# A head's values times both halves of its probabilities: one matmul of 512 columns in place of two of 256, and a sum on VectorE

## What is computed

```python
kv_input = jnp.concatenate([xn, ln], axis=1)
k, v = jnp.split(kv_input @ Wkv + bkv, 2, axis=-1)
sim = jnp.einsum('bhid,bhjd->bhij', q * DH ** (-0.5), k)
attn = jax.nn.softmax(sim, axis=-1)
out = jnp.einsum('bhij,bhjd->bhid', attn, v)
return out.transpose(0, 2, 1, 3).reshape(b, -1, INNER) @ Wo + bo
```

## Time and profile before

| | us |
|---|---|
| median of three runs | 1913.81 |
| profiled execution | 1916.26 |
| its span, first to last instruction | 1914.4 |
| TensorE busy | 1889.9 (99%) |
| VectorE busy | 1464.6 (77%) |
| ScalarE busy | 1221.6 (64%) |
| GpSimd busy | 392.2 (20%) |
| first half of the program | to about 1075 |

### The profile page before, as it was taken

The page is one execution under the profiler, slowest core; times in us unless marked ns, Lnnn a source line. Parts: engine busy times, 40 slices in busy tenths (PEclk is TensorE's granted clock), DMA queues, the critical chain, the costliest instruction groups (busy, mean ns, idle before and its releaser), DMA issues.

```text
span 1914.4 us, 41535 instructions
## 1 busy us (share of the span) xinstructions
PE 1889.9 (99%) x13834; PEld 1764.6 (92%) x13834; DVE 1464.6 (77%) x3620; ACT 1221.6 (64%) x2554; POOL 392.2 (20%) x610
## 2 busy tenths in 40 slices
PE   7999999999999999999999999999999999999999
PEld 6888888888888888888889899999999999999998
DVE  7877777777777776777667788888888878888776
ACT  5655565556555655565566776667777777767753
POOL 2222222222222222122255211111111111111100
PEclk9999999999999999999999999999999999999999
DMA  3021112111210000000052933433333333433400
GB/s 125 29 72 40 43 60 71 38 44 60 71 38 28 12 22 22 11 11 22 13 109 53 332 79 80 84 59 82 85 72 75 76 71 75 85 75 66 86 7 12
DMA packets 101982, 119.33 MB, mean 62 GB/s; under 512 B 39072, under 2 KB 87072, under 8 KB 101920
## 3 DMA queue, kind: packets, MB, share of 16 engines
q1 hardware_dynamic: 93216, 83.93, 14.5%
q0 software_dynamic: 8704, 34.61, 10.0%
HBM read 97.29 MB, written 21.23 MB: 62 GB/s over the span
## 4 chain that ended last, share of the span: by engine, by line
PE 93%; DVE 3%; ACT 2%; DMA 1%; issue 1%; POOL 0%; DVEq 0%; SPq 0%; POOLq 0%; ACTq 0%
PE ring L651 10%; PE ring L653 10%; PE ring L652 10%; PE ring L1935 8%; PE ring L1937 8%; PE ring L1936 8%; PE ring L707 5%; PE sim L651 3%; PE sim L653 3%; PE sim L1937 3%; PE sim L652 3%; PE sim L1935 3%; PE sim L1936 3%; PE ps_x L651 1%; PE ps_x L652 1%; PE ps_x L653 1%
## 5 line engine op out<-in xcount | busy, mean ns | idle before, releaser
L435 ACT ACTIVATE a_pr<-sim,a_nmax 128x512 f32<-128x512 f32 x256 | 173.8, 684 | 204.9 <-DVE a_nmax L566 204.9
L1935 PE MATMUL ring<-b_xch,b_wel 128*128 128x256 f32 x1024 | 289.9, 283 | 0.5 <-DVE b_act_e L1558 0.5
L1937 PE MATMUL ring<-b_xcl,b_weh 128*128 128x256 f32 x1024 | 286.5, 280 | 0.0
L1936 PE MATMUL ring<-b_xch,b_weh 128*128 128x256 f32 x1024 | 286.3, 280 | 0.0
L346 POOL TENSOR_SCALAR a_pr<-a_pr,a_rinv 128x512 f32<-128x512 f32 x256 | 185.0, 739 | 450.8 <-DVE a_rinv L576 448.0
L1936 PEld LDWEIGHTS ring<-b_xch,b_weh 128*128 128x128 f32 x1024 | 193.4, 189 | 0.0
L1935 PEld LDWEIGHTS ring<-b_xch,b_wel 128*128 128x128 f32 x1024 | 192.1, 188 | 0.7 <-DVE b_act_e L1558 0.7
L1937 PEld LDWEIGHTS ring<-b_xcl,b_weh 128*128 128x128 f32 x1024 | 192.1, 188 | 0.0
L1274 ACT ACTIVATE b_heh<-b_act_e 128x512 fp32r<-128x512 f32 x128 | 80.7, 630 | 147.0 <-DVE b_act_e L1558 113.1
L544 DVE SCALAR_TENSOR_TENSOR a_ktl<-ring,a_bkv_s,a_kth 128x512 fp32r<-128x512 f32 x128 | 95.3, 745 | 96.7 <-ACT a_kth L415 95.9
L557 DVE TENSOR_TENSOR a_ptl<-ring,a_pth 128x512 fp32r<-128x512 f32 x256 | 163.8, 681 | 1.6 <-ACT a_pth L425 0.5
(11 more groups left out here) (357 smaller groups left out, 6345.2 us busy)
## 6 DMA issues: line engine op xcount, KB each, us to landing
b_w2l_raw<-in_W2T POOLq DMA_DIRECT2D x16, 1088.0 KB, 8.6
b_even_b<-rows_between SPq DMA_DIRECT2D x16, 1024.0 KB, 5.5
b_w1l_raw<-in_W1T POOLq DMA_DIRECT2D x16, 1024.0 KB, 8.3
b_w1l_raw<-in_We SPq DMA_DIRECT2D x8, 768.0 KB, 4.5
expert_halves<-b_w1h SPq DMA_DIRECT2D x8, 768.0 KB, 3.3
expert_halves<-b_w1l SPq DMA_DIRECT2D x8, 768.0 KB, 5.6
b_weh<-expert_halves SPq DMA_DIRECT2D x8, 768.0 KB, 7.3
b_wel<-expert_halves SPq DMA_DIRECT2D x8, 768.0 KB, 8.9
```

What stands on the lines that cost most here:

```text
L435: nc.scalar.activation(pr[:, h % 2, t, :], sim[t][:], ACT.Exp, bias=nmax[:, h % 2, t:t + 1], accum_out=rsum[:, h % 2, t:t + 1]).then_inc(e ...
L1935: nc.tensor.matmul(out, ll, rh, start=(n == 0), stop=False)
L1936: nc.tensor.matmul(out, lh, rh, start=False, stop=False)
L1937: last = nc.tensor.matmul(out, lh, rl, start=False, stop=(n == len(parts) - 1))
```

## The change

The tiles `pth` and `ptl` become the two parts of one tile `pt` (P x 2 x 4 x 256). In the O fill, for each block k, `vh` is multiplied with both parts in one matmul of 512 columns into the whole bank, so that `vh x pth` lies in columns 0 to 255 and `vh x ptl` in columns 256 to 511; `vl x pth` is still a matmul of 256 columns and is added to the first part. VectorE's low half of O then has two instructions: the old one from the first part, and a sum that adds the second part to `otl`, after a wait for the first (a new semaphore `o_step`, counted up to 128).

```diff
-    pth, ptl = (of["probs"].put(n, [P, KT, S], F32R, odd=0) for n in ("a_pth", "a_ptl"))
+    pt = of["probs"].put("a_pt", [P, 2, KT, S], F32R, odd=0)
+    pth, ptl = pt[:, 0], pt[:, 1]
-    consts = sem("consts")
+    consts, o_step = sem("consts"), sem("o_step")
-        def low_half(order, i):
+        def low_half(order, i, heads=0):
             else:
                 nc.vector.scalar_tensor_tensor(otl[:, h], bank[:, 0:S], bkv_s[:, 1, h:h + 1], f32(oth[:, h]),
-                                               ALU.add, ALU.subtract).then_inc(ring_lo, 1)
+                                               ALU.add, ALU.subtract).then_inc(o_step, 1)
+                dve.wait_ge(o_step, heads)
+                nc.vector.tensor_tensor(otl[:, h], f32(otl[:, h]), bank[:, S:2 * S], ALU.add).then_inc(ring_lo, 1)
-                    low_half(order, i + j)
+                    low_half(order, i + j, b * H + h)
-                low_half(order, i)
+                low_half(order, i, b * H + H)
-                last = product(bank[:, 0:S], range(KT), lambda k: vh[h // KT][:, k, cols],
-                               lambda k: vl[h // KT][:, k, cols], lambda k: pth[:, k, :], lambda k: ptl[:, k, :])
+                wide = bank[:].rearrange("p (z s) -> p z s", z=2)
+                for k in range(KT):
+                    left = vh[h // KT][:, k, cols]
+                    if k > 0:
+                        nc.tensor.matmul(bank[:, 0:S], vl[h // KT][:, k, cols], pth[:, k, :], start=False, stop=False)
+                    last = nc.tensor.matmul(wide, left, pt[:, :, k, :], start=(k == 0), stop=(k == KT - 1))
+                    if k == 0:
+                        nc.tensor.matmul(bank[:, 0:S], vl[h // KT][:, k, cols], pth[:, k, :], start=False, stop=False)
```

## The result

The changed kernel takes 1922.51 us (median of 5 runs, 1922.11 to 1922.84), the one before 1914.66 us in the same comparison (1913.24 to 1915.64). The ratio is 1.0043 with an interval of 1.0032 to 1.0053: slower, by 7.9 us of the medians. The profiled execution took 1922.57 us with a span of 1920.8 us, 6.4 us more than that of before; TensorE's granted clock has a mean of 0.999 (0.998 before), so the clock did not make it slower.

What follows compares the result with a forecast made beforehand. TensorE, busy 1889.9 of 1914.4 us, sets the time. Turn 0 0.8, turns 1 to 8 6.2, turns 9 to 13 1.8, turn 14 0.4, last turn 1.0, matmuls 0.5: +10.7 on 1913.8 gives 1924.5 us, range 1914 to 1935.

Steps and rivals of the forecast that it cites:

- The matmuls, +0.5 us: TensorE's O fills: one 512-column matmul costs what two of 256 cost; +0.5 us in all, ends -1 and +2.6.
- d = 0.43 us a head: VectorE's low half of O: wait and sum add 0.43 us per head, 55 us in all; bounds 0.30 and 0.56.
- Absorbed in slots 0 to 2 and 7: In these head slots of a turn VectorE's idle time takes up the delay; about 0.13 us is left in slot 2.
- Slot 4, d - 0.08 a turn: O's low half in slot 4 delays TensorE's loads, less 0.08 us idle: 0.35 us in each of turns 9 to 13.
- Slot 3, another d in turns with split: Turns 1 to 8, splitting expert weights: no idle time in slot 3, so with slot 4 they lose 0.78 us each.
- Turn 0, +0.8: First turn: loses 0.8 us, taken to be like the turns with a weight split.
- Turn 14, +0.4: The turn before the last: adds 0.4 us.
- The last turn, +1.0: Last turn, interleaved with the second half: between 0 and 3.4 us, taken as 1.0.
- (a): Rival: longer VectorE chain, 0.56 us per head, more slots bind, 1934 us; chance 0.16.
- (b): Rival: the wide TensorE matmul takes 216 ns, gaining 7.7 us, while the stall stays; 1916 us; chance 0.07.
- (d): Rival: weight loads bind TensorE's stream, wide matmuls save 7.7 us and stalls are absorbed; 1906 us; chance 0.06.
- (c): Rival: idle time elsewhere absorbs the delay in slots 3 and 4, needing 0.43 us idle; 1914 us; chance 0.11.

Runs made afterwards that it cites:

- e1: Changed kernel with its merged matmuls but without VectorE's sum and the wait for it (output incomplete): 1914.29 us, ratio 1.0004 to the kernel before.
- e2: Changed kernel with twelve 256-column matmuls again, those of ptl into the bank's second part, wait and sum kept: 1922.14 us, ratio 1.0044 to the kernel before.
- e4: Kernel before, with wide matmuls, wait and sum for head 3 alone: 1917.82 us, ratio 1.0022 to the kernel before.
- e5: Changed kernel with head 3's sum put off until after the next maxima, in turns that prepare a next one: 1919.38 us, ratio 1.0029 to the kernel before.
- e6: Changed kernel with one more GpSimd instruction of about 0.40 us ahead of the residual sum in slot 3: 1924.87 us, ratio 1.0055 to the kernel before.
- b1: Kernel before, with slot 5's reciprocals moved behind the second keys' halves (L512, L514): 1910.50 us, ratio 0.9985 to the kernel before.
- a1: Changed kernel with slot 5's reciprocals moved behind the second keys' halves: 1919.73 us, ratio 1.0032 to the kernel before.
- e3: Changed kernel, but head 3 keeps the old narrow matmuls and has no sum: 1917.36 us, ratio 1.0022 to the kernel before.

## Why the prediction was right, and where its steps were not

The predicted time was 1924.5 us, +10.7 over before; measured are +7.9 by the medians and +6.4 by the spans. The direction and the mechanism held. The term for slot 3 was 3.4 us too large, and the last turn's was too small by 0.5 to 2.1 us, so the two errors partly cancel: that the total came this near is in part luck. By its steps:

- *The matmuls, +0.5 us.* Right within what can be told, if anything too low. e1 gives +0.8 us, and e2 against the changed kernel 0.4 us the other way. From an O fill's first matmul of 256 columns to the next fill's first the changed kernel takes 1.39 to 1.41 us, above the 1.36 to 1.38 that the text gives as a sign; the kernel before took 1.36 to 1.42, depending on the fill behind. Over the eight fills of a turn (385 to 446 us before) the means are 1.40 and 1.38 us, a loss of 0.14 us a turn, part of which the wait before the scores takes up (3.3 us in e1 for 3.9). A merged matmul of 512 columns holds the stream no shorter than two of 256. In the changed kernel's O fill the wide one at 403.80 is followed by the next after 0.24 us, a narrow one by the wide one after 0.11:

```profile
403.69 0.28 PE L721 MATMUL ring<-a_pt,a_vl 128*128 128x256 f32 x1
403.80 0.40 PE L722 MATMUL ring<-a_pt,a_vh 128*128 128x512 f32 x1
404.04 0.28 PE L721 MATMUL ring<-a_pt,a_vl 128*128 128x256 f32 x1
```

  The signs in the text can be read as 1024 matmuls of 256 columns after the change. There are 512 of 512 columns and 512 of 256, 1024 in all; 13834 - 13322 = 512 instructions went.
- *d = 0.43 us a head.* Right: 0.86 us from start to start, where it was 0.39 to 0.43. The sum takes 420 to 424 ns in all 128 cases, as estimated from the halved widths; that is 53.8 us:

```profile
L565 DVE TENSOR_TENSOR a_otl<-a_otl,ring x128: 420/421/424, 40.8 to 1074.6; 128x256 fp32r<-128x256 f32 x128
```

- *Absorbed in slots 0 to 2 and 7.* Right, and on a larger scale than the text says: VectorE's wait for V shrank by 36.6 us.
- *Slot 4, d - 0.08 a turn.* Right in kind. The waits at the two places together grew from 0.66 to 0.90 us in turns with split, by 0.24 (the text expected some 1.4), and the matmuls add up to 0.1; turns 9 to 13 lost 0.32 us by the marks above, where 0.35 was predicted. e4 shows head 3's sum to be the cause, e5 its place in the queue.
- *Slot 3, another d in turns with split.* This is the step that failed. The text took the split's 1.16 us as a fixed length and let the full d reach TensorE. In fact the split starts 0.40 us later against GpSimd's residual sum (1.07 us after its start, 0.67 before), runs beside it for a shorter time, and ends where it ended before. So these turns lose 0.32 us by the marks, not 0.78; from one mark of slot 5 to the next (581.61 before, 585.38 after; in turn 0 they are 0.93 apart) 3.77 - 0.93 = 2.8 us for eight turns, where 6.2 were predicted. That is 3.4 us of the sum. e6 takes the cover away, and the split, the second wait and about 2.4 of these 3.4 us come back.
- *Turn 0, +0.8.* Measured 0.93 us. Here no step was costed by itself; the agreement isn't a test.
- *Turn 14, +0.4.* Measured -1.1 us, in the profiled executions: the two kernels' weight loads that wait for the low half of K

```profile
944.86 0.42 PEld L707 LDWEIGHTS ring<-ident,a_pr 128*128 128x128 f32 x4 [2.38 <-DVE a_ktl L544]
```

```profile
948.96 0.42 PEld L711 LDWEIGHTS ring<-ident,a_pr 128*128 128x128 f32 x4 [1.16 <-DVE a_ktl L546]
```

  wait 2.38 and 1.16 us. Ahead of that low half VectorE waits for the second half's first rows to land:

```profile
940.42 0.42 DVE L1515 BATCH_NORM_STATS2 b_row_stats<-b_first_rows 32x6 f32<-32x256 f32 x1 [2.70 <-DMA b_first_rows<-x_between]
```

```profile
944.52 0.42 DVE L1525 BATCH_NORM_STATS2 b_row_stats<-b_first_rows 32x6 f32<-32x256 f32 x1 [1.51 <-DMA b_first_rows<-x_between]
```

  The load was issued at 936.44 and 942.20, so it was in VectorE's hands 4.0 us after its issue in the one and 2.3 in the other. The profiled execution of before lay 1.6 us over the median of its runs and that of the changed kernel at its median, and the two spans differ by 1.5 us less than the medians. A load that landed late in that one execution accounts for both, and the other traces bear it out: in all eight of them it was in VectorE's hands 2.4 to 2.6 us after its issue. b1 differs from the kernel before by two statements exchanged in slot 5; its rows here, with the load issued at 932.75:

```profile
935.33 0.42 DVE L1515 BATCH_NORM_STATS2 b_row_stats<-b_first_rows 32x6 f32<-32x256 f32 x1 [1.30 <-DMA b_first_rows<-x_between]
```

```profile
939.77 0.42 PEld L707 LDWEIGHTS ring<-ident,a_pr 128*128 128x128 f32 x4 [0.98 <-DVE a_ktl L544]
```

  From the load before the scores of slot 4 in turn 13 to that in turn 14 it is 66.27 us in the trace of before, but 64.75 in e1 (899.26, 964.01) and in b1 (895.38, 960.13), 65.39 in the changed kernel (904.18, 969.57) and 65.47 in a1 (900.89, 966.36). So a turn 14 costs 0.64 us by the one pair and 0.72 by the other, where 0.4 was predicted, and the -1.1 us belongs to one late load. Why it was late is not shown.
- *The last turn, +1.0.* Measured 2.2 us, inside its 0 to 3.4: the first half ends at 1088.56 before and 1094.85 after, 6.29 apart, of which 4.10 stood at turn 14's wait. Counted from slot 4 of turn 14 on it is 1.5 us against e1 (125.28 us for 123.75) and 3.1 for a1 against b1 (125.29 for 122.19): a step too small by 0.5 to 2.1 us. One row of it is a wait that was 0.47 us for L560, another the longest for T's low half, 1.16 us before:

```profile
997.31 0.19 PEld L655 LDWEIGHTS ps_x<-a_woh,a_otl 128*128 128x128 f32 x1 [0.92 <-DVE a_otl L565]
...
1071.82 0.19 PEld L722 LDWEIGHTS ring<-a_pt,a_vh 128*128 128x128 f32 x1 [1.66 <-DVE a_pt L559]
```

- *The rivals.* (a) fell with d = 0.43. (b) and (d) fell with e1 and e2: no width is cheaper. (c) is nearly true of seven heads of eight, as far as turns 1 to 13 go (0.04 to 0.09 us a turn in e3), though in slot 3 of turns with split by the shorter split and not by idle time. It is not true of head 3, where the idle time of 0.43 us that it needed does not exist.

The 3 us that e3 loses outside turns 1 to 13 lie at the end: its turn 0 is within 0.1 us of the kernel before's (70.62 and 70.55 at the load for the keys' input), its turn 14 is 65.25 us (900.03, 965.28), 0.5 over e1 and b1, and what follows to the end of the first half (1090.51) takes 125.23 us, 1.5 and 3.0 more than in these two. What is not settled is which waits make up the last turn's 1.5 to 3.1 us.

## What to carry to other kernels

Cost an added instruction by the slot where it stands, not by its engine's busy share: here seven of eight sums together cost about as much as the one behind which the next scores were waiting. Merging matmuls along their columns saved nothing here, where start to start goes by columns (232 ns for 512, 113 for 256); check the seams before paying for it on another engine. And a duration in a full chain is fixed only if nothing runs beside it: where a shift moves a two-operand VectorE instruction against GpSimd's, cost it again, and look for such collisions in the kernel as it stands, since the move that undid one here was worth 3.4 us, and the merging nothing that could be measured.

## What the runs showed of the hardware

In these traces a VectorE instruction with both inputs in SBUF, the core's on-chip memory, is held up by GpSimd instructions beside it. GpSimd's residual sum of the kernel before, and of the changed one:

```profile
440.55 1.29 POOL L353 TENSOR_TENSOR a_x_res<-a_x_res,a_bo_b 128x512 f32<-128x512 f32 x1
```

```profile
443.37 1.29 POOL L354 TENSOR_TENSOR a_x_res<-a_x_res,a_bo_b 128x512 f32<-128x512 f32 x1
```

They end at 441.84 and 444.66, the one of e6 at 447.87. The splits, started at 441.22, 444.44 and 447.28, end at 442.38, 445.20 and 448.42: 0.54, 0.54 and 0.55 us after GpSimd's end, whenever they began. Those of e3 and e4 (above) fit too, with 0.54 and 0.55 us. Undisturbed a split takes 0.68 us. It looks as if most of its work, 0.54 of 0.68 us, waits until GpSimd is done. GpSimd's own 1.29 us hardly changed (1.31 in e6), and it was the first to start in all three; in slot 5, where the two scalings surround L514, both sides paid (1.07 us for 0.69, and 1.98 for 1.37). The sum, whose second input lies in PSUM, the memory that the matmuls write, never varied (420 to 424 ns), although in 100 of its 128 cases one of GpSimd's scalings ran beside it: the one at 49.11 us lies wholly within the pair of scalings from 48.41 to 49.78.

The Trainium skill, "SBUF — State Buffer", Who interferes with whom, says that a VectorE instruction with two SBUF inputs contends with a GpSimd instruction that reads SBUF, and one with at most one SBUF input, outside the modes that use two ports, does not. By that rule both numbers agree: the split and L514 have two such inputs, the sum has one.
